# Attention denominators through VectorE and DRAM, and output products of 128 tokens, in a cross-attention kernel on one core

## What is computed

```python
a = layer_norm(ctx, gamma, beta)
Q, K, V = x @ Wq.T, a @ Wk.T, a @ Wv.T            # split in 16 heads of 32
attn = softmax(where(mask, Q K^T / sqrt(32), -inf))
return x + tanh(gate) * ((attn @ V) @ Wo.T)
```

## Time and profile before

| | before |
|---|---|
| median of 3 runs | 940.44 us (939.95 to 940.76) |
| the profiled execution | 940.45 us |
| its span | 938.4 us |
| TensorE busy | 928.2 us, 99% |
| VectorE busy | 706.4 us, 75% |
| ScalarE busy | 685.8 us, 73% |
| GpSimd busy | 639.4 us, 68% |
| DMA packets | 85850, 105.54 MB |
| chain that ended last, TensorE's share | 95% |

### The profile page before, as it was taken

One profiled execution on the slowest core, in us unless ns is written; L12 is line 12 of the kernel. 1 busy time (PEld: TensorE's weight loads), 2 busy tenths in 40 slices (PEclk: granted clock), 3 DMA queues, 4 the chain that ended last, 5 costly groups with the idle time before them and its releaser, 6 DMA issues.

```text
span 938.4 us, 26747 instructions
## 1 busy us (share of the span) xinstructions
PE 928.2 (99%) x10723; PEld 805.9 (86%) x10723; DVE 706.4 (75%) x1381; ACT 685.8 (73%) x1296; POOL 639.4 (68%) x724
## 2 busy tenths in 40 slices
PE   9999999999999999999999999999999999999997
PEld 8898888888888888888888888888888888888885
DVE  6972498778777778777877777877787777887677
ACT  3422687777778787787877778777787777878775
POOL 0672366777777777777777777877777777777765
PEclk9999999999999999999999999999999999999999
DMA  9983143334344433444434443344443443334212
GB/s 280 344 266 150 29 101 93 92 104 115 90 98 113 111 92 88 104 113 116 105 85 111 115 107 82 93 111 114 115 98 90 113 114 95 91 94 113 56 39 59
DMA packets 85850, 105.54 MB, mean 112 GB/s; under 512 B 22528, under 2 KB 63488, under 8 KB 85728
## 3 DMA queue, kind: packets, MB, share of 16 engines
q1 hardware_dynamic: 85152, 102.93, 41.3%
q10 hardware_dynamic: 576, 0.92, 0.3%
HBM read 86.39 MB, written 17.43 MB: 111 GB/s over the span
## 4 chain that ended last, share of the span: by engine, by line
PE 95%; DMA 1%; DVE 1%; ACT 1%; SPq 0%; issue 0%; DVEq 0%
PE banks L959 66%; PE banks L1104 10%; PE banks L1117 8%; PE banks L982 7%; PE banks L1123 2%; DMA shared_f<-in_xT 1%; ACT shared_q L630 0%; ACT shared_q L639 0%; DMA x_odd<-row_stats 0%; DVE shared_q L865 0%; PE banks L1085 0%; DVE shared_r L751 0%; PE banks L990 0%; SPq L319 0%; ACT shared_f L644 0%
## 5 line engine op out<-in xcount | busy, mean ns | idle before, releaser
L959 PE MATMUL banks<-shared_r,w_k 128*128 128x376 f32 x1536 | 291.7, 339 | 0.6 <-ACT shared_f L680 0.5
L630 ACT ACTIVATE shared_q<-banks,maskT,rstd 125x448 f32<-125x448 f32 x384 | 243.4, 729 | 55.3 <-PE banks L1104 55.0
L959 PE MATMUL banks<-w_v,shared_r 128*125 128x512 f32 x1152 | 283.5, 395 | 0.0
L855 DVE TRANSPOSE_TENSOR_REDUCE rmax<-shared_q 128x14 f32<-128x448 f32 x384 | 219.8, 625 | 82.3 <-ACT shared_q L630 81.1
L959 PEld LDWEIGHTS banks<-shared_r,w_k 128*128 128x128 f32 x1536 | 263.1, 188 | 13.5 <-issue 0.9
L493 POOL TENSOR_TENSOR shared_f<-shared_q 125x448 f32<-125x448 f32 x124 | 142.0, 1145 | 163.7 <-PE banks L1123 163.2
L959 PEld LDWEIGHTS banks<-w_v,shared_r 128*125 128x125 f32 x1152 | 212.9, 186 | 44.5
L865 DVE TENSOR_TENSOR shared_q<-shared_q,banks 125x448 f32<-125x448 f32 x384 | 208.2, 607 | 0.1
L639 ACT ACTIVATE shared_q<-shared_q 125x448 f32<-125x448 f32 x384 | 186.4, 568 | 2.5 <-DVE shared_q L865 2.5
L497 POOL TENSOR_TENSOR shared_f<-shared_f,shared_q 125x448 f32<-125x448 f32 x124 | 142.3, 1148 | 9.7
L461 POOL TENSOR_TENSOR shared_r<-cn,shared_r 128x375 fp32r<-128x375 f32 x124 | 112.3, 927 | 42.9 <-ACT shared_r L591 42.8
(11 more groups left out here) (93 smaller groups left out, 785.1 us busy)
## 6 DMA issues: line engine op xcount, KB each, us to landing
cn<-in_ctxT SPq DMA_DIRECT2D x128, 187.5 KB, 4.0
rows<-in_ctx SPq DMA_DIRECT2D x32, 720.0 KB
xy<-in_x SPq DMA_DIRECT2D x32, 224.0 KB, 7.4
q_kept<-shared_q SPq DMA_DIRECT2D x8, 896.0 KB, 7.5
shared_q<-q_kept SPq DMA_DIRECT2D x32, 224.0 KB, 3.9
out<-xy SPq DMA_DIRECT2D x32, 224.0 KB, 3.8
shared_f<-in_xT SPq DMA_DIRECT2D x7, 896.0 KB, 11.3
x<-row_stats SPq DMA_DIRECT2D x64, 84.0 KB
```

The costliest lines, as they stand in the source:

```text
L630: act.activation(prob[0:SP_, n % NB, j, :] .rearrange("p (a h t) -> p a h t", a=2, h=2), score_view(n, j), ACT.Identity, bias=maskT[0:SP_, ...
L855: last = dve.tensor_reduce(rmax[:, n % 2, BLK * j:BLK * j + BLK], prob[:, n % NB, j, :].rearrange("p (k a) -> p k a", a=32), AX.X, ALU.max ...
L959: last = pe.matmul(dst, l, m, start=(start and k == 0), stop=(stop and k == len(pairs) - 1))
```

## The change

For batches 0 to 28 (`SUMMED` = 29) TensorE makes no denominators. In their place:

1. VectorE's `partial_sums(p)` reduces each slot's summed exponentials within blocks of 32 partitions by one transposing reduction; `sum_chunks` waits for it before it writes a buffer again. Both stand for slots 2m-4 and 2m-3, the partial sums at the end of VectorE's pair.
2. SP stores the parts of a batch to DRAM at the head of even pairs and loads them back on 32 partitions behind the maxima's loads.
3. VectorE's `shares(b)`, at the end of even pairs, adds the four parts, inverts and transposes.
4. SP stores the shares at the head of odd pairs, and loads them by four DMAs, each copying its rows to 32 partitions, into `rshare`, behind the maxima's loads.
5. GpSimd's `normalised` multiplies by `rshare`, for batch c - 3 now in even pairs; `high_half` and `low_half` move with it to even pairs of c, on ScalarE between K out and V out, on GpSimd behind `add_bias`.

`oT` becomes a ring of 256 columns, and the output product takes 128 of them: 28 products (tiles) in place of 32. `tile_of(b)` gives the tile whose product is made in the pair of batch b, and none for b a multiple of 8. Where a batch crosses the ring's end, `high_half` and `low_half` are two instructions each. Loads of x, stores and additions go by tiles of 128 rows. The last three batches keep their denominators on TensorE.

```diff
+TILES = B * T // 128
+RING = 256
...
-        at, oT = cut_r(at, 2, KT, T)
+        at, oT = cut_r(at, 2, KT, RING)
...
+        SUMMED = B - 3
...
+        def tile_of(b):
+
+            return b - 1 - b // 8 if 0 <= b < B and b % 8 else None
+
+        def tiles(b):
+
+            return b - b // 8 if b > 0 else 0
+
+        def pieces(b):
+
+            at = b * T % RING
+            n = min(T, RING - at)
+            return [(0, at, n)] + ([(n, 0, T - n)] if n < T else [])
+
+        def sums_of(b):
+            return pv[:, b % 2 * HT:b % 2 * HT + HT].rearrange("p (c t) -> p c t", c=KT)
...
+            def store_parts(b):
+                need(sync, ld_parts, 16 * b)
+                sync.wait_ge(part_done, b * KT + KT)
+                sync.dma_start(bass.AP(tensor=part_kept.tensor, offset=0,
+                                       ap=[[HT // 8, HC], [HC * HT // 8, 32], [1, HT // 8]]),
+                               parts[:, :]).then_inc(parts_stored, 16)
+
+            def load_parts(b):
+                sync.wait_ge(parts_stored, 16 * b + 16)
+                need(sync, whole_done, b)
+                sync.dma_start(part4[:, :], part_kept.rearrange("a q k -> a (q k)")) \
+                    .then_inc(ld_parts, 16)
+
+            def store_shares(b):
+                need(sync, ld_shares, 64 * b)
+                sync.wait_ge(share_done, b + 1)
+                sync.dma_start(share_kept.rearrange("(i r) a -> r i a", i=2),
+                               share_rows[:, :].rearrange("r (i a) -> r i a", i=2)) \
+                    .then_inc(shares_stored, 16)
+
+            def load_shares(b):
+                sync.wait_ge(shares_stored, 16 * b + 16)
+                need(sync, o_norm, b)
+                for h in range(HC):
+                    sync.dma_start(rshare[HD * h:HD * h + HD, :].rearrange("p (u t) -> p u t", u=KT),
+                                   bass.AP(tensor=share_kept.tensor, offset=T * h,
+                                           ap=[[0, HD], [HT, KT], [1, T]])) \
+                        .then_inc(ld_shares, 16)
+
+            def summed(b):
+                return 0 <= b < SUMMED
+
             for m in range(PAIRS):
                 c, odd = divmod(m, 2)
+                if summed(c - 2):
+                    if odd:
+                        store_shares(c - 2)
+                    else:
+                        store_parts(c - 2)
                 store_maxima(2 * m)
                 store_maxima(2 * m + 1)
                 load_maxima(2 * m)
                 load_maxima(2 * m + 1)
+                if summed(c - 2):
+                    if odd:
+                        load_shares(c - 2)
+                    else:
+                        load_parts(c - 2)
...
             def normalised(b):
-                pool.wait_ge(rspread_done, b + 1)
                 o = pv[:, b % 2 * HT:b % 2 * HT + HT]
-                pool.tensor_tensor(o, o, rspread[:, :], ALU.mult).then_inc(o_norm, 1)
+                if b < SUMMED:
+                    pool.wait_ge(ld_shares, 64 * b + 64)
+                    pool.wait_ge(pv_out, b * KT + KT)
+                    pool.tensor_tensor(o, o, rshare[:, :], ALU.mult).then_inc(o_norm, 1)
+                else:
+                    pool.wait_ge(rspread_done, b - SUMMED + 1)
+                    pool.tensor_tensor(o, o, rspread[:, :], ALU.mult).then_inc(o_norm, 1)
 
             def low_half(b):
                 pool.wait_ge(o_hi, b + 1)
-                pool.tensor_tensor(oT[:, 1, :, :].rearrange("p c t -> p (c t)"),
-                                   pv[:, b % 2 * HT:b % 2 * HT + HT],
-                                   oT[:, 0, :, :].rearrange("p c t -> p (c t)").bitcast(F32),
-                                   ALU.subtract).then_inc(o_done, 1)
+                for t, at, n in pieces(b):
+                    last = pool.tensor_tensor(oT[:, 1, :, at:at + n], sums_of(b)[:, :, t:t + n],
+                                              oT[:, 0, :, at:at + n].bitcast(F32), ALU.subtract)
+                last.then_inc(o_done, 1)
 
             def sum_chunks(p):
 
                 q, h = p % NB, p % 2
                 pool.wait_ge(exp_done, p * ST + 2)
-                need(pool, pv_mm, p - 1)
+                if p - 2 < SUMMED * KT:
+                    need(pool, part_done, p - 1)
+                else:
+                    pool.wait_ge(pv_mm, p - 1)
...
-                if odd and 1 < c < B - 1:
-                    low_half(c - 2)
                 if not odd and m >= 0:
-                    if c > 1:
-                        normalised(c - 2)
+                    if c > 2:
+                        normalised(c - 3)
+                        if tile_of(c - 3) is not None:
+                            add_bias(tile_of(c - 3))
+                        low_half(c - 3)
+                    if m == PAIRS - 2:
+                        normalised(B - 3)
                     if c + 1 < B and c > 0:
                         row_statistics(c + 1)
-                    if c > 2:
-                        add_bias(c - 3)
-                if odd and c > 2:
-                    result(c - 3)
+                if odd and tile_of(c - 3) is not None:
+                    result(tile_of(c - 3))
...
             def high_half(b):
                 act.wait_ge(o_norm, b + 1)
-                need(act, y_mm, b)
-                act.activation(oT[:, 0, :, :].rearrange("p c t -> p (c t)"),
-                               pv[:, b % 2 * HT:b % 2 * HT + HT], ACT.Copy).then_inc(o_hi, 1)
-
-            def gated_out(b, at=VO):
-                act.wait_ge(y_mm, b + 1)
-                need(act, y_done, b)
-                act.activation(gated[0:T, :], bank[at][0:T, :], ACT.Copy, scale=gat[0:T, 0:1]) \
+                need(act, y_mm, (b * T - RING + T - 1) // 128 + 1)
+                for t, at, n in pieces(b):
+                    last = act.activation(oT[:, 0, :, at:at + n], sums_of(b)[:, :, t:t + n], ACT.Copy)
+                last.then_inc(o_hi, 1)
+
...
             def weighted_out(p, b=KB):
 
                 act.wait_ge(pv_mm, p + 2)
-                if p % KT == 0 and p > 0:
-                    act.wait_ge(dsum_done, p // KT)
+                if p == (B - 2) * KT:
+                    act.wait_ge(dsum_done, 1)
                 if p % KT == 0 and p > KT:
                     act.wait_ge(o_done, p // KT - 1)
+                if p < SUMMED * KT:
+                    act.wait_ge(sum_done, p + 2)
+                    at = p % 8 * T
+                    act.activation(pv[:, at:at + 2 * T], bank[b][:, 0:2 * T], ACT.Copy) \
+                        .then_inc(pv_out, 2)
+                    return
...
-                if odd and 1 < c < B - 1:
-                    high_half(c - 2)
...
+                if not odd and c > 2:
+                    high_half(c - 3)
...
+            def partial_sums(p):
+                dve.wait_ge(sum_done, p + 1)
+                if p % KT == 0:
+                    need(dve, parts_stored, p // KT * 16)
+                u = p % KT
+                dve.tensor_reduce(parts[:, BLK * u:BLK * u + BLK],
+                                  psum[:, p % 2, :].rearrange("p (k a) -> p k a", a=32),
+                                  AX.X, ALU.add, apply_transpose=True).then_inc(part_done, 1)
+
+            def shares(b):
+                dve.wait_ge(ld_parts, 16 * b + 16)
+                n = KT * BLK
+                dve.tensor_reduce(whole_sum[:, 0:n], part4[:, :].rearrange("p (q k) -> p k q", q=HC),
+                                  AX.X, ALU.add).then_inc(whole_done, 1)
+                dve.wait_ge(whole_done, b + 1)
+                dve.reciprocal(whole_sum[:, 0:n], whole_sum[:, 0:n]).then_inc(share_step, 1)
+                dve.wait_ge(share_step, b + 2)
+                need(dve, shares_stored, 16 * b)
+                dve.transpose(share_rows[:, :], whole_sum[:, :]).then_inc(share_done, 1)
...
-                if not odd and c > 1:
-                    normalise(c - 2)
+                if m == PAIRS - 2:
+                    normalise(B - 3)
...
+                for p in (2 * m - 4, 2 * m - 3):
+                    if 0 <= p < SUMMED * KT:
+                        partial_sums(p)
+                if not odd and 0 <= c - 2 < SUMMED:
+                    shares(c - 2)
...
             def output(b, behind_v, at=VO):
                 pe.wait_ge(o_done, b + 1)
                 pe.wait_ge(v_done, behind_v)
-                product(bank[at][0:T, :],
-                        [(oT[:, a, k, :], wo[:, d, k, :])
+                at_row = 128 * tile_of(b) % RING
+                product(bank[at],
+                        [(oT[:, a, k, at_row:at_row + 128], wo[:, d, k, :])
                          for k in range(KT) for a, d in PASSES]).then_inc(y_mm, 1)
...
                     for j in range(ST):
-                        weighted(p + q, j, to[:, q * T:q * T + T])
+                        last = weighted(p + q, j, to[:, q * T:q * T + T])
+                if p < SUMMED * KT:
```

(21 more changed lines are left out.)

125 lines of the change are left out of this document (77 added, 48 removed).

## The result

The changed kernel takes 972.8 us (970.4 to 977.2, four runs) against 940.6: ratio 1.0347, interval 1.0308 to 1.0386. I had forecast 922.3, between 906 and 936, and gave slower 8%. The profiled execution took 972.34 us with a span of 970.5.

What follows compares the result with a forecast made beforehand. Pairs with an output product were taken as bound by PE, those without by ACT. Savings of 28.8 us less 4.0, 2.0 and 4.7 gave 18.1 off 940.45: 922.3 us, range 906 to 936.

Steps and rivals of the forecast that it cites:

- (a): Denominators of batches 0 to 28 leave TensorE: 0.39 us saved a pair, 20.3 over 52 ordinary pairs.
- (b): 28 output products for 32: four odd pairs fall to ACT's 11.07 us, 2.0 saved each, denominators included; 128 tokens cost as 112.
- VectorE's added work: Four partial sums at 0.65 us each or some 0.6 in a row, and shares at 1.15, between 0.45 and 1.75.
- issued at 7.3: SP issues load_parts 7.3 us after an even pair's first scores_out, behind the odd maxima's load; it lands at 11.1.
- the wait 1.3: VectorE stands 1.3 us in even pairs until the parts' load lands.
- R2: Rival: mild stall per batch from dearer shares or parts' load delays low_half; 3 to 20 us, 924 to 940; chance 0.25.
- D: In R2, low_half's lateness after its 0.7 us of slack: 0.2 to 1.5 us, about half staying on 27 batches.
- R3: Rival: shares' load releases the whole chain and delays PE's output; slower, 968 if it takes 7.4 us; chance 0.08.
- two signs of being wrong: PE waiting in each batch ahead of the output, or POOL waiting for the shares; no size given.
- (c): After five short odd pairs, VectorE's unmoved schedule makes PE wait for its bank: 0.8 us each, 4.0 lost.
- (d): That lag is passed on once, by the partial sum, to the next batch's output: 0.5 us x 4, 2.0 lost.
- (e): Tail: last pair's output product waits for batch 28's normalised, add_bias and low_half: 4.7 us lost.

Runs made afterwards that it cites:

- denom_only: Changed kernel with denominators alone, SP in the order of heads, and one output product of 112 rows per batch: 926.3 us, 0.985 of the kernel before.
- ring_only: Changed kernel with the ring alone: 28 output products of 128 tokens, all denominators on TensorE, halves in the earlier order: 932.8 us, 0.992 of the kernel before.
- heads: Changed kernel with the loads of parts and shares each moved right behind their own store, at the pair's head: 922.7 us, 0.981 of the kernel before.
- parts_mid: From heads: parts' load between the maxima's stores and loads in even pairs, batch 28's normalised and halves moved earlier: 909.5 us, 0.967 of the kernel before.

## Why the prediction was wrong, point by point

- **(a), denominators, 0.39 a pair: right.** The step from the weighted sums to the scores keeps its cost: in after the 48 matmuls ahead of the scores take 1.28 between their start and the scores', where they took 1.17 ahead of denominators, 0.11 more. TensorE's timeline of after:

```profile
487.79 1.36 PE L1248 MATMUL banks<-shared_q,shared_f 125*32 125x112 f32 x48
489.07 1.19 PE L1235 MATMUL banks<-shared_q,shared_f 32*125 32x112 f32 x30
```


  The border stays when the denominators go, then. The Trainium skill (TensorEngine Tiling (Array Packing), Key Properties) says that changing the tiling mode drains TensorE, and the 0.11 agrees with it. The pairs of denom_only are 12.69 and 12.70.
- **(b), output products: right and slightly low.** Short pairs are 10.9 to 11.0 where I had 11.07; 156.51 - 145.04 less 0.47 is 11.0, so that part of the miss is my arithmetic. A product for 128 tokens costs 0.07 less than one for 112, not the same (ring_only's odd pairs are 13.02 for 13.08).
- **VectorE's added work: right.** Partial sums take 0.6 (two in 1.17, the row of 500.81), and shares 1.36 (506.40 to 507.76) where I took 1.15, between 0.45 and 1.75.
- **The step that failed: load_parts "issued at 7.3", with "it spends most of a pair waiting for maxima, and the context loads behind have a pair to land".** The 7.3 is an issue time of the kernel before, and in it lies that kernel's time from the maxima's store to their load, 2.2 to 2.5 us, with the rows' loads no nearer than 7.2 us ahead. I carried it over as a constant. I counted SP's new issues by their issue time and asked whether the loads behind them would be in time, but not what these loads, 3 us later in the queue, would stand in front of. With the rows 2.6 us ahead the same store took 6.2. The 7.3 became 11.7 (502.58 less scores_out at 490.84), and the wait 1.3 became 3.7. R2 had the right load and the right waiter, and a D of 1.5 at most; its 3 to 20 us on 922.3 also make 925 to 942, not 924 to 940. R3 had the right kind of mechanism on the wrong load: I looked for a large transfer ahead of the shares and found none, and didn't look for one ahead of the maxima's stores. The shares were never waited for on GpSimd, and ahead of the output product TensorE waited 7.8 us in 15 waits, 4.4 of them in the tail, so that neither of my two signs of being wrong came. It waited 24.8 us ahead of the scores.
- **(c) and (d), lag after short pairs: wrong in cause.** I gave it to VectorE's work, 6.0 us in all. In heads the pairs behind a short one are 12.67 to 13.34, in parts_mid 12.66 or 12.67, with the same work on VectorE, so that this work alone makes no lag. In heads what is left of it hangs on SP's stand at the parts' store: behind short pair 39 the rows are issued at 569.28, `load_parts` at 578.63, the maxima's stores at 579.04, and VectorE waits for maxima; pair 40 takes 13.34.
- **(e), the tail: right in place and size of the gap** (forecast 4.7 us, 4.36 in after and 4.37 in heads), **too small in all** (7.0), since TensorE's clock fell over the wait, which my sum had no term for. TensorE's timeline of the last pair in after:

```profile
934.97 4.41 PE L1090 MATMUL banks<-w_o,shared_r 128*128 128x512 f32 x12 [4.36 <-POOL shared_r L575]
```

GpSimd's, the same stretch:

```profile
931.47 1.13 POOL L567 TENSOR_TENSOR shared_f<-shared_f,rshare 128x448 f32<-128x448 f32 x1
932.56 1.27 POOL L553 TENSOR_TENSOR xy<-xy,gbo 128x512 f32<-128x512 f32 x1
933.79 1.13 POOL L575 TENSOR_TENSOR shared_r<-shared_f,shared_r 128x448 fp32r<-128x448 f32 x1
```

`normalised`, `add_bias`, `low_half` and then the output product stand in a row as I had them. The product takes 4.41 us here and 5.49 in heads, in place of 2.96. In heads the windows ahead of the wait, of the wait and of the product have these granted clocks:

```profile
874.00:879.00 5.00, 5.00 (x124) 4.72 (x124) 0.89 (x2) 3.40 (x7) 3.21 (x3) 1.00 0.07 22
879.50:883.80 4.30, 0.00 (x0) 0.00 (x0) 2.22 (x5) 2.55 (x5) 4.30 (x5) 0.88 0.00 0
883.80:889.40 5.60, 5.55 (x13) 4.39 (x14) 5.60 (x12) 0.02 (x1) 1.09 (x1) 0.50 0.10 18
```

- **The sum itself** comes out close to heads, 922.7 measured for 922.3. That is partly luck, since two misses cancel: its tail was 2.3 too small, and for pairs 6 to 62 its terms give 21.9 us (51 x 0.39 + 8.0 - 6.0) where heads gained 24.1, mostly by the products' 0.07 each. And heads isn't the kernel that I forecast.

## What to carry to other kernels

When a change adds DMA issues to an in-order queue, write down for every transfer behind them what it will be issued in front of, and price the small round trip that follows at the time to drain those bytes (here some 9 us from the issue of 750 KB and its neighbours), not at its time in an idle queue. Keep a load whose reader waits within the same stage out from behind other round trips, and away from bulk loads; a late transfer costs nothing where its reader has slack. Loading back right behind its own store helps as long as the queue doesn't stand there: heads had the parts so, and parts_mid, with that load a step further back, was 6 us faster in the ordinary pairs. The same change was 3.5% slower or 3.3% faster by the place of the parts' and the shares' loads on SP and of one batch's tail.

## What I had not expected of the hardware

- From the store of 21 KB of maxima to the issue of the load that waits for it: 2.5 us with nothing large issued in the 7 us before, 6.9 with 1.4 MB issued in the 3 us before; 4.9 with 750 KB issued on ScalarE's queue 1.9 us before. From the rows' issue to that load it is 8.8 us in after (median; 7.8 to 10.3), however close behind them the store stands.
- TensorE's granted clock over and behind a wait of 4.4 us: 1.00 (the 2.4 GHz level) ahead of it, 0.88 over it, 0.50 (the 1.2 GHz level) over the product that ended it, which took 5.49 us in place of 2.96. That is 2.5 us on top of the wait's own 4.4.
- A shorter wait does it too. Behind the 1.95 us in after that end at 518.04, with the engine busy before them, the granted clock is 1.00 up to 518, 0.57 from there to 519, 0.50 to 521, 0.72 to 522 and 1.00 again from there; the K product of 519.95 took 3.06 us where it takes 2.3.
- Twelve matmuls with 128 stationary columns took 2.89 us against 2.96 with 112 (the output products of ring_only and before), and an odd pair of ring_only is 13.02 against 13.08.
- Cutting four loads from 32 partitions to one didn't make the kernel faster: one execution took 986.1 us, for 970.4 to 977.2. The rows then stood 2.0 us ahead of the stores in nearly every batch; why isn't shown.
